# A selective-scan layer with routed experts: a second PSUM bank for the output projection, and turned y in the bank of the inputs' product

## Chip, cores and metric

One core of a Trainium2 chip runs the whole program. The time is the device time in microseconds of one execution, and what is compared is the median of several runs.

## The reference

The input x has 8 sequences of 1024 tokens of 128 features. After a layer norm, a Mamba-2 layer and a mixture of experts read the same normalised xn, and both are added to x. The part that the change touches is the Mamba-2 layer:

```
zxbcdt = norm(xn) @ W_in.T                      # z 256, x 256, B 128, C 128, dt 4 columns
xBC = silu(causal conv with 4 taps of xBC)
Y_diag, states, Y_off = chunked scan over tokens
Y = Y + xs * D                                  # "skip"
y = Y * silu(z)                                 # "gate"
y = y * rsqrt(mean(y * y) + eps) * rms_w
out = y @ W_out.T                               # "output projection"
x = x + (xn + out) + experts(xn)
```

The kernel uses chunks of 128 tokens, so there are 64 tiles of 128 tokens, 8 in each sequence.

## The kernel before

Each engine has its own hand-written program, and semaphores join them. After a prologue (norms, routing, first projection) comes the scan, from about 100 to 490 us, then the experts (500 to 705 us) and the final sum. The scan runs over 8 sequences with a loop for sequences 1 to 6; in each, `sequence(b)` runs over j = 0 to 7, one tile nn = 8b + j each. Four tiles are a group (g = j // 4, q = j % 4): the input projection, convolution and Silu are made for 512 tokens at once, for the next group, while the scan works on the present one.

What the engines do for a tile, in order:

- TensorE: `exponents` (L781, L782) builds the decay exponents in bank 2; `project` (L771) makes one of six blocks of the next group's input projection in bank 0; `front` (L790, L792) the product of B and C and three transposes; `project_out` (L825, L827) multiplies the gated y of tile nn-3 by W_out and sums its squares, all in bank 7; `middle` (L806, L809, L810) makes both parts of y in bank 5 and the inputs' product in the first half of bank 6; `turn_y` (L817) transposes y of tile nn-1 into bank 1. At q = 3 there is no projection, and `project_out` comes first.
- VectorE: `outputs` (L1164, L1167, L1169; L1171 and L1172 for j = 0) takes y and state out of banks 5 and 6; `skip` (L1189) adds D times x to the turned y of tile nn-2; `gate` (L1199) multiplies by silu(z); `by_token` makes `xb` (L1149) and the masked product `m_sb` (L1153); between them lie the other three convolution taps of the next group (L1076), where the table FILL puts them. `outputs` of tile j-1 is called in the quarter of tile j, except that at q = 3 both j-1 and j are done.
- ScalarE: `keep_out` (L604, L605) copies the output projection and the sum of squares out of bank 7 for tile nn-4; `decays` (L566) is the exponential of the exponents; `row` (L597) the row for the experts; `keep_proj` (L534) and `tap0` (L541) copy the projection and make the first tap; `square` (L609) squares the gated y. At the end of q = 2 come `keep_out` of tile nn-3 and then `silu` (L552 to L561), with a load of the activation table on either side.
- POOL scales the inputs (`xde`, L428) and the state (`state_k`, L463) and scatters rows to memory.

Two orders matter. `project_out` waits until the output of the tile before has been copied out of bank 7 (`o_kept`), so at q = 3 and q = 0 it waits for ScalarE's copies on either side of Silu. And `middle` waits for `y_done` of the tile before and for `xde_done`, since it overwrites banks 5 and 6.

Of the kernel before, what the change touches and what calls it, by code (L numbers as in the profile page):

```python
# [27 lines left out]
P = 128  # L28
# [33 lines left out]
def program(nc, x, ln_w, ln_b, w_in_t, w_dt, conv_w, conv_b, dt_bias, a_log, d_skip, rms_w, w_out_t,  # L62
            router, gate_w, up_w, down_w, out):
    ctx = ExitStack()
    with ctx:  # L65
# [3 lines left out]
        def sem(name):  # L69
# [143 lines left out]
        ms_done, rms_sq, rms_done, resid_done, place_free, total_done = (sem(n) for n in (  # L213
            "ms_done", "rms_sq", "rms_done", "resid_done", "place_free", "total_done"))

        def by_head(t):
# [270 lines left out]
        def _(act_e):  # L487
# [111 lines left out]

            def keep_out(nn):  # L600
                act_e.wait_ge(norm_done, 2)
                act_e.wait_ge(o_done, nn + 1)
                act_e.wait_ge(xn_done, nn + 1)
                A(x_sb[:, tile_ix(nn), :].rearrange("p a d -> p (a d)"), bank[7][:, 0:D], ACT.Copy)  # L604
                A(ssq[:, tile_ix(nn)], bank[7][:, D:D + 1], ACT.Copy).then_inc(o_kept, 1)  # L605

# [4 lines left out]
            def sequence(b):  # L611
                first, last = is_first(b), is_last(b)
                for j in range(SC):
                    nn, q, g = b * SC + j, j % GC, j // GC
                    more = not (last and g == 1)
                    nxt, g6 = b * 2 + g + 1, (b * 2 + g + 1) * NAT
                    if q < 3 and not (first and j < 4):
                        keep_out(nn - 4)
# [12 lines left out]
                    if more and q == 2:  # L631
                        keep_proj(g6, 5, 1 - g)
                    if not (first and j < 2):
                        square(nn - 2, j % 2)
                    if more and q == 0:
                        keep_proj(g6, 2, 1 - g)
                    if more and q == 1:
                        tap0(g6, 2, 1 - g)
                        tap0(g6, 3, 1 - g)
                        keep_proj(g6, 4, 1 - g)  # L640
                    if q == 2:
                        if not last:
                            act_e.wait_ge(taps_done, nxt * NCT * HALO + 2 * HALO)
                            halo(nxt + 1, g, 0)
                            keep_proj(g6 + NAT, 0, g)
                            act_e.wait_ge(front_done, nn + 2)
                            tap0(g6 + NAT, 0, g)
                        if more:
                            act_e.wait_ge(m_done, nn + 1)
                            decays(nn + 2, j % 2)  # L650
                        if not (first and j < 4):
                            keep_out(nn - 3)
                        if more:
                            silu(nxt, 1 - g)
                    if last and g == 1 and q:
                        weights_high(q - 1)
# [10 lines left out]
            weights_high(3)  # L667
            keep_out(NT - 4)
            keep_out(NT - 3)
            for n_ in (NT - 2, NT - 1):  # L670
                square(n_, n_ % 2)
            for n_ in (NT - 2, NT - 1):
                keep_out(n_)
            act_e.wait_ge(ms_done, 1)
# [30 lines left out]
        def _(pe):  # L705
# [89 lines left out]
            def middle(b, j):  # L795
# [4 lines left out]
                else:  # L800
                    pe.wait_ge(y_done, nn)
                    if j % GC == 0:
                        pe.wait_ge(m_done, nn + 1)
# [7 lines left out]

            def turn_y(nn, u, early):
                pe.wait_ge(y_done, nn + 1)
                if not early:
                    pe.wait_ge(skip_done, nn)
                for c in range(2):
                    tp = nc.tensor.transpose(bank[1][:, c * P:(c + 1) * P], y_sb[:, u, c * P:(c + 1) * P], ident[:, :])  # L817
                tp.then_inc(yt_done, 1)

            def project_out(nn, u, early):  # L820
                pe.wait_ge(sq_done, nn + 1)
                if not early:
                    pe.wait_ge(o_kept, nn)
                for c in range(2):
                    mm(bank[7][:, 0:D], yg[:, u, c * P:(c + 1) * P], wo_sb[:, c, :], start=(c == 0), stop=(c == 1))  # L825
                for c in range(2):
                    m = mm(bank[7][:, D:D + 1], sq[:, u, c * P:(c + 1) * P], ones[:, 0:1], start=(c == 0),  # L827
                           stop=(c == 1))
# [16 lines left out]
            def sequence(b):  # L845
                first, last = is_first(b), is_last(b)
                for j in range(SC):
# [10 lines left out]
                    if more and q:  # L858
                        project(*nxt, 2 * q + 1)
                    if not (first and j < 3):  # L860
                        project_out(nn - 3, (j - 3) % 2, first and j < 4)
                    if q == 2 and not (last and g == 1):
# [4 lines left out]
                    if not (first and j < 1):  # L867
                        turn_y(nn - 1, (j - 1) % 2, first and j < 2)
                    if ahead and q == 3:
# [5 lines left out]
            project_out(NT - 3, (NT - 3) % 2, False)  # L875
            turn_y(NT - 1, (NT - 1) % 2, False)
            project_out(NT - 2, (NT - 2) % 2, False)
# [65 lines left out]
        def _(dve):  # L943
# [213 lines left out]
            def outputs(b, j):  # L1157

                nn, u, later = b * SC + j, j % 2, b * (SC - 1) + j
                dve.wait_ge(mid_done, nn + 1)  # L1160
                if j:
                    if not (is_first(b) and j == 1):
# [19 lines left out]
            def skip(nn, j):  # L1182
# [5 lines left out]
                for c in range(2):  # L1188
                    sk = V.scalar_tensor_tensor(out=yd_sb[:, c * P:(c + 1) * P], in0=ab[:, XT0 + c, cs],  # L1189
                                                scalar=ds_c[:, c:c + 1], in1=bank[1][:, c * P:(c + 1) * P],  # L1190
                                                op0=ALU.mult, op1=ALU.add)
                sk.then_inc(skip_done, 1)

            def gate(nn, j, group):
                ab, cs, u = group_act(j // GC), in_group(j), j % 2
                dve.wait_ge(skip_done, nn + 1)
                if j % GC == 0:
                    dve.wait_ge(gate_silu, group + 1)
# [13 lines left out]
            def sequence(b):  # L1212
                first, last = is_first(b), is_last(b)
                for j in range(SC):
# [127 lines left out]
```

## Time and profile before

| | |
|---|---|
| median of 3 runs | 753.68 us (751.95 to 761.06) |
| profiled execution | 749.04 us, of which the span of instructions is 747.2 us |
| mean granted TensorE clock | 0.957 |
| busy, share of the span | PE 81%, DVE 77%, ACT 63%, POOL 57% |
| busiest group on DVE | L1076, convolution taps, 192 instructions, 147.6 us |
| chain that ended last | PE 26%, nearly all of it in the experts (L908, L936, L925) |

The trace names the engines PE (TensorE), DVE (VectorE), ACT (ScalarE) and POOL (GpSimd). PEld is TensorE's load of weights. The chain that ended last is followed back from the end and reaches the experts, not the scan; for the scan one has to read waits and timelines.

### The profile page before, as it was taken

How to read it: one execution, taken by the hardware profiler on the slowest of the kernel's cores; microseconds unless marked ns; L12 is line 12 of the kernel's file. 1: busy time of each engine (PE TensorE's matmuls, PEld its weight loads, DVE VectorE, ACT ScalarE, POOL GpSimd, SP SyncE). 2: the span in 40 equal slices, each digit the busy share in tenths (PEclk: the TensorE clock that was granted, in tenths of full speed). 3: DMA queues.
4: the chain of work that ended last, by engine and by line, in shares of the span. 5: the costliest groups of instructions: out<-in, count | busy, mean ns of one | idle time of the engine just before them, and what ended most of it. 6: DMA issues, size and time to landing. Idle time of an engine off the chain costs nothing. (4 is left out here: it accounts for less than half of the span.)

```text
span 747.2 us, 15261 instructions
## 1 busy us (share of the span) xinstructions
PE 608.8 (81%) x3702; PEld 516.1 (69%) x3703; DVE 577.9 (77%) x1440; ACT 470.5 (63%) x1014; POOL 425.8 (57%) x622
## 2 busy tenths in 40 slices
PE   0696448888998999999899988769999999999700
PEld 0696226677877777877777777658898888888600
DVE  7676998998988989889889898766666667666354
ACT  0254355788778887788877887446666666666400
POOL 4343006677767667676777657705666666666710
PEclk9999999999999999899999999979999999999955
DMA  9980000000000000000000003333333333332179
GB/s 304 268 174 0 26 6 17 26 26 29 24 26 27 24 23 23 23 26 27 23 23 27 23 24 111 111 89 105 107 113 105 105 105 109 107 106 81 43 289 385
DMA packets 64651, 61.48 MB, mean 82 GB/s; under 512 B 9242, under 2 KB 55710, under 8 KB 64624
## 3 DMA queue, kind: packets, MB, share of 16 engines
q1 hardware_dynamic: 56176, 44.11, 20.6%
q0 software_dynamic: 8448, 17.06, 6.7%
q8 instruction: 11, 0.18, 0.1%
q14 instruction: 16, 0.13, 0.1%
HBM read 30.19 MB, written 31.47 MB: 83 GB/s over the span
## 5 line engine op out<-in xcount | busy, mean ns | idle before, releaser
L479 POOL DMA_INDIRECT moe_d<-raw,slot_st x136 | 133.7, 983 | 91.9 <-issue 69.4
L452 POOL DMA_INDIRECT slots_d<-rows,slot_st x128 | 135.9, 1062 | 74.1 <-POOL rows L447 52.8
L1076 DVE SCALAR_TENSOR_TENSOR act<-raw,taps,act 128x512 f32<-128x512 f32 x192 | 147.6, 776 | 16.6 <-ACT act L541 15.8
L680 ACT ACTIVATE l_sb<-bank 128x256 f32<-128x256 f32 x136 | 44.8, 381 | 73.2 <-PE bank L908 73.2
L428 POOL TENSOR_TENSOR xde<-xb,e_end 128x256 f32<-128x256 f32 x64 | 48.1, 751 | 62.6 <-DVE xb L1149 61.3
L1264 DVE CAST x_hi<-bank 128x256 fp32r<-128x256 f32 x68 | 28.9, 425 | 64.0 <-PE bank L917 64.0
L806 PE MATMUL bank<-xb,m_sb 128*128 128x64 f32 x512 | 71.4, 285 | 6.5 <-POOL xde L428 4.4
L806 PEld LDWEIGHTS bank<-xb,m_sb 128*128 128x128 f32 x512 | 66.7, 200 | 8.3 <-issue 4.6
L936 PE MATMUL bank<-act,raw 128*128 x544 | 71.9, 275 | 0.0
L936 PEld LDWEIGHTS bank<-act,raw 128*128 128x128 f32 x544 | 66.1, 192 | 0.2 <-issue 0.2
L908 PE MATMUL bank<-xw_hi,x_hi 128*128 x136 | 59.9, 440 | 6.0 <-DVE m_sb L1275 6.0
L825 PE MATMUL bank<-wo_sb,yg 128*128 128x128 f32 x256 | 41.9, 287 | 26.1 <-ACT tok L605 25.7
L534 ACT ACTIVATE raw<-bank,proj_b 128x512 f32<-128x512 f32 x64 | 44.0, 688 | 25.7 <-PE bank L771 22.8
L825 PEld LDWEIGHTS bank<-wo_sb,yg 128*128 128x128 f32 x256 | 36.1, 193 | 34.3 <-issue 20.7
L771 PE MATMUL bank<-xw_hi,w_hi 128*128 (+1 forms) x96 | 51.9, 540 | 5.6 <-ACT raw L534 3.2
L541 ACT ACTIVATE act<-raw,cols,taps 128x512 f32<-128x512 f32 x64 | 50.2, 807 | 8.6 <-DVE meta L1140 5.8
L609 ACT ACTIVATE sq<-yg 128x256 f32<-128x256 f32 x64 | 26.3, 410 | 44.3 <-DVE yg L1199 44.2
L908 PE MATMUL bank<-xw_lo,x_hi 128*128 x136 | 53.9, 396 | 0.0
L908 PE MATMUL bank<-xw_hi,x_lo 128*128 x136 | 53.8, 395 | 0.0
L1153 DVE TENSOR_TENSOR m_sb<-l_sb,bank 128x512 f32<-128x512 f32 x64 | 43.4, 678 | 0.0
L1164 DVE TENSOR_TENSOR yo_sb<-bank,e_cs 128x256 f32<-128x256 f32 x56 | 23.4, 417 | 25.2 <-PE bank L810 25.2
L566 ACT ACTIVATE l_sb<-bank 128x512 f32<-128x512 f32 x64 | 38.2, 597 | 6.6 <-PE bank L782 6.5
(233 smaller groups left out, 1692.8 us busy)
## 6 DMA issues: line engine op xcount, KB each, us to landing
slots_d<-rows SPq DMA_DIRECT2D x8, 1122.0 KB, 13.6
rows<-slots_d SPq DMA_DIRECT2D x68, 132.0 KB, 2.2
x_sb<-in_x SPq DMA_DIRECT2D x8, 512.0 KB, 6.4
act<-in_x SPq DMA_DIRECT2D x64, 64.0 KB
xw_hi<-moe_d SPq DMA_DIRECT2D x8, 512.0 KB, 9.1
xw_lo<-moe_d SPq DMA_DIRECT2D x8, 512.0 KB, 9.8
out<-x_sb SPq DMA_DIRECT2D x8, 512.0 KB, 13.3
moe_d<-raw,slot_st POOLq DMA_INDIRECT x136, 2.3
```

The lines of the kernel that those rows point to most:

```text
L428: nc.gpsimd.tensor_tensor(by_head(xde[:, u, :]), by_head(xdt[:, u, :]), per_head(e_end, nn), ALU.mult).then_inc(xde_done, 1)
L452: nc.gpsimd.indirect_dma_start(out=slots_d, out_offset=bass.IndirectOffsetOnAxis(ap=slot_st[:, r, c:c + 1], axis=0), in_=rows[:, r, c, :], ...
L479: nc.gpsimd.indirect_dma_start(out=moe_d, out_offset=bass.IndirectOffsetOnAxis(ap=slot_st[:, r, c:c + 1], axis=0), in_=ym[r % R][:, c * D: ...
L534: A(proj[:, t, HALO:] if t < NCT else group_act(par)[:, t, :], bank[0][:, :], ACT.Identity, bias=proj_b[:, t:t + 1]).then_inc(proj_done, 1)
L541: A(group_act(par)[:, t, :], proj[:, t, HALO:], ACT.Identity, bias=cb_c[:, t:t + 1], scale=taps[:, t, HALO:]).then_inc(tap0_done, 1)
L680: a = A(l_sb[:, r % 2, c * F:(c + 1) * F], bank[2 + 2 * (r % 2) + c][:, 0:F], ACT.Silu)
L771: m = mm(bank[0][:, :], w[:, c], v[:, bass.ds(b * SW + PADW + half * GT, GT)], start=(a == 0), stop=(a == 2))
L806: mm(bank[5][:, h * HD:(h + 1) * HD], m_sb[:, u, h * P:(h + 1) * P], xdt[:, u, h * HD:(h + 1) * HD], start=True, stop=True)
L825: mm(bank[7][:, 0:D], yg[:, u, c * P:(c + 1) * P], wo_sb[:, c, :], start=(c == 0), stop=(c == 1))
L908: gu = mm(bank[2 + 2 * (r % 2) + c][:, :], xs[:, r % 2, c * P:(c + 1) * P], w[:, bass.ds(ex[c] * (2 * F), 2 * F)], start=(a == 0), stop=(a ...
L936: o = mm(bank[1 + 6 * (r % 2)][:, c * D:(c + 1) * D], ht[r % 2][:, (2 * c + f) * P:(2 * c + f + 1) * P], dn_sb[:, bass.ds(ex[c] * (2 * D) ...
L1076: V.scalar_tensor_tensor(out=group_act(par)[:, t, :], in0=proj[:, t, k:k + GT], scalar=taps[:, t, k:k + 1], in1=group_act(par)[:, t, :], o ...
```

## The change

It gives the output projection two banks, 7 and 1, taken in turn by the parity of the tile, so that `project_out` waits for the copy of the tile two before. Bank 1 came from `turn_y`, whose transposes now go to the second half of bank 6, beside the inputs' product. Since a bank must not be written by TensorE while VectorE reads it, `middle` now waits for `skip` of tile nn-2, `outputs` waits for `turn_y` of the tile before, and `gate` names its wait for the projection that read its buffer. At q = 0 `project_out` moves behind `middle` and `turn_y`, and the `skip` of that quarter moves to the quarter before, between `xb` and the masked product. On ScalarE the copy that stood before Silu moves behind it, after the square.

```
+        out_ps = (bank[7], bank[1])
+        yt_ps = bank[6][:, DI:2 * DI]
...
-            def keep_out(nn):
+            def keep_out(nn, u):
...
-                A(x_sb[:, tile_ix(nn), :].rearrange("p a d -> p (a d)"), bank[7][:, 0:D], ACT.Copy)
+                A(x_sb[:, tile_ix(nn), :].rearrange("p a d -> p (a d)"), out_ps[u][:, 0:D], ACT.Copy)
...
                     if not (first and j < 2):
                         square(nn - 2, j % 2)
+                    if q == 3 and not (first and j < 4):
+                        keep_out(nn - 4, j % 2)
...
-                        if not (first and j < 4):
-                            keep_out(nn - 3)
                         if more:
                             silu(nxt, 1 - g)
...
                     pe.wait_ge(y_done, nn)
+                    if not (is_first(b) and j < 2):
+                        pe.wait_ge(skip_done, nn - 1)
...
-                    tp = nc.tensor.transpose(bank[1][:, c * P:(c + 1) * P], y_sb[:, u, c * P:(c + 1) * P], ident[:, :])
+                    tp = nc.tensor.transpose(yt_ps[:, c * P:(c + 1) * P], y_sb[:, u, c * P:(c + 1) * P], ident[:, :])
...
-                    pe.wait_ge(o_kept, nn)
+                    pe.wait_ge(o_kept, nn - 1)
...
-                    mm(bank[7][:, 0:D], yg[:, u, c * P:(c + 1) * P], wo_sb[:, c, :], start=(c == 0), stop=(c == 1))
+                    mm(out_ps[u][:, 0:D], yg[:, u, c * P:(c + 1) * P], wo_sb[:, c, :], start=(c == 0), stop=(c == 1))
...
-                    if not (first and j < 3):
-                        project_out(nn - 3, (j - 3) % 2, first and j < 4)
+                    if q and not (first and j < 3):
+                        project_out(nn - 3, (j - 3) % 2, first and j < 5)
...
                     middle(b, j)
                     if not (first and j < 1):
-                        turn_y(nn - 1, (j - 1) % 2, first and j < 2)
+                        turn_y(nn - 1, (j - 1) % 2)
+                    if not q and not (first and j < 3):
+                        project_out(nn - 3, (j - 3) % 2, first and j < 5)
...
                 dve.wait_ge(mid_done, nn + 1)
+                if not (is_first(b) and j < 1):
+                    dve.wait_ge(yt_done, nn)
...
                 dve.wait_ge(skip_done, nn + 1)
+                if not isinstance(nn, int) or nn > 1:
+                    dve.wait_ge(o_done, nn - 1)
...
-                    if not (first and j < 2):
+                    if q and not (first and j < 2):
                         skip(nn - 2, (j - 2) % SC)
...
-                    if not (last and j == SC - 1):
+                    if q < 3:
                         by_token(b, j + 1, lambda: fill(2))
+                    elif not (last and j == SC - 1):
+                        by_token(b, j + 1, lambda: skip(nn - 1, j - 1))
+                        fill(2)
```

## Rows read from the trace of the kernel before

**Rows 1.** Busy time by stretch; columns: stretch, PE, PEld, DVE, ACT, POOL, clock, DMA.
```profile
180.00:230.00 50.00, 45.87 (x294) 38.25 (x294) 44.13 (x96) 41.93 (x85) 35.15 (x59) 1.00 0.08 25
```

**Rows 2.** Waits, 180.14 to 271.75 us, four groups: total us, times, longest.
```profile
ACT sq L609 <- DVE yg L1199: 8.5, 8, 1.8
PE bank L825 <- ACT tok L605: 7.6, 8, 1.5
...
DVE act L1076 <- ACT act L541: 4.5, 8, 0.7
DVE yo_sb L1164 <- PE bank L810: 4.5, 4, 1.1
...
ACT raw L534 <- PE bank L771: 3.8, 8, 1.0
```

**Rows 3.** ScalarE's timeline, table load before Silu: start us, length us.
```profile
180.14 1.28 ACT L552 ACT_TABLE_LOAD   x1
...
271.75 1.28 ACT L552 ACT_TABLE_LOAD   x1
295.91 1.28 ACT L552 ACT_TABLE_LOAD   x1
...
436.25 1.28 ACT L552 ACT_TABLE_LOAD   x1
```

**Rows 4.** ScalarE's timeline through one group; in brackets the idle time before.
```profile
245.90 0.42 ACT L609 ACTIVATE sq<-yg 128x256 f32<-128x256 f32 x1 [1.29 <-DVE yg L1199]
...
257.10 0.81 ACT L541 ACTIVATE act<-raw,cols,taps 128x512 f32<-128x512 f32 x1
```

**Rows 5.** VectorE's timeline through the same group.
```profile
248.84 0.41 DVE L1169 TENSOR_TENSOR y_sb<-yo_sb,bank 128x256 f32<-128x256 f32 x1
249.17 0.60 DVE L1189 SCALAR_TENSOR_TENSOR yd_sb<-act,cols,bank 128x128 f32<-128x128 f32 x2
...
252.01 0.42 DVE L1164 TENSOR_TENSOR yo_sb<-bank,e_cs 128x256 f32<-128x256 f32 x1 [1.12 <-PE bank L810]
...
254.14 0.68 DVE L1153 TENSOR_TENSOR m_sb<-l_sb,bank 128x512 f32<-128x512 f32 x1
...
257.94 1.56 DVE L1076 SCALAR_TENSOR_TENSOR act<-raw,taps,act 128x512 f32<-128x512 f32 x2 [0.41 <-ACT act L541]
...
261.68 0.50 DVE L1199 TENSOR_TENSOR yg<-yd_sb,act 128x256 f32<-128x256 f32 x1
```

**Rows 6.** TensorE's timeline: the first group's q = 3, then the same group.
```profile
132.95 1.10 PE L806 MATMUL bank<-xb,m_sb 128*128 128x64 f32 x8 [1.02 <-DVE y_sb L1169]
...
248.98 0.68 PE L825 MATMUL bank<-wo_sb,yg 128*128 128x128 f32 x4 [0.95 <-ACT tok L605]
...
249.86 1.08 PE L806 MATMUL bank<-xb,m_sb 128*128 128x64 f32 x8
...
251.27 0.59 PE L810 MATMUL bank<-xde,xb 128*128 128x256 f32 x2
251.70 0.38 PE L817 MATMUL bank<-ident,y_sb 128*128 128x128 f32 x2
...
255.28 0.71 PE L825 MATMUL bank<-wo_sb,yg 128*128 128x128 f32 x4 [0.66 <-ACT tok L605]
...
256.20 1.08 PE L806 MATMUL bank<-xb,m_sb 128*128 128x64 f32 x8
...
257.75 0.48 PE L771 MATMUL bank<-xw_hi,w_hi 128*128 x1
```

**Rows 7.** POOL's timeline: inputs scaled for the first tile of a group.
```profile
253.75 0.95 POOL L428 TENSOR_TENSOR xde<-xb,e_end 128x256 f32<-128x256 f32 x1 [0.69 <-DVE xb L1149]
```

**Rows 8.** TensorE's timeline and stretch (clock ahead of the last two), slow group; tail.
```profile
272.76 1.62 PE L806 MATMUL bank<-xb,m_sb 128*128 128x64 f32 x8
...
274.00:278.00 4.00, 4.00 (x16) 3.07 (x16) 1.65 (x5) 3.97 (x7) 1.65 (x2) 0.68 0.11 34
...
489.98 1.19 PE L825 MATMUL bank<-wo_sb,yg 128*128 128x128 f32 x4 [0.57 <-ACT tok L605]
```

More of the change, by code:

```diff
@@ L603, in keep_out @@
                 act_e.wait_ge(xn_done, nn + 1)
-                A(x_sb[:, tile_ix(nn), :].rearrange("p a d -> p (a d)"), bank[7][:, 0:D], ACT.Copy)
-                A(ssq[:, tile_ix(nn)], bank[7][:, D:D + 1], ACT.Copy).then_inc(o_kept, 1)
+                A(x_sb[:, tile_ix(nn), :].rearrange("p a d -> p (a d)"), out_ps[u][:, 0:D], ACT.Copy)
+                A(ssq[:, tile_ix(nn)], out_ps[u][:, D:D + 1], ACT.Copy).then_inc(o_kept, 1)
             def square(nn, u):
@@ L617, in sequence @@
                     if q < 3 and not (first and j < 4):
-                        keep_out(nn - 4)
+                        keep_out(nn - 4, j % 2)
                     if q < 3:
@@ L634, in sequence @@
                         square(nn - 2, j % 2)
+                    if q == 3 and not (first and j < 4):
+                        keep_out(nn - 4, j % 2)
                     if more and q == 0:
@@ L667, in _ @@
             weights_high(3)
-            keep_out(NT - 4)
-            keep_out(NT - 3)
+            keep_out(NT - 4, 0)
+            keep_out(NT - 3, 1)
             for n_ in (NT - 2, NT - 1):
@@ L672, in _ @@
             for n_ in (NT - 2, NT - 1):
-                keep_out(n_)
+                keep_out(n_, n_ % 2)
             act_e.wait_ge(ms_done, 1)
@@ L810, in middle, with turn_y @@
                 mm(bank[6][:, 0:DI], b_sb[:, u, :], xde[:, u, :], start=True, stop=True).then_inc(mid_done, 1)
-            def turn_y(nn, u, early):
+            def turn_y(nn, u):
                 pe.wait_ge(y_done, nn + 1)
-                if not early:
+                if not isinstance(nn, int) or nn > 0:
                     pe.wait_ge(skip_done, nn)
                 for c in range(2):
-                    tp = nc.tensor.transpose(bank[1][:, c * P:(c + 1) * P], y_sb[:, u, c * P:(c + 1) * P], ident[:, :])
+                    tp = nc.tensor.transpose(yt_ps[:, c * P:(c + 1) * P], y_sb[:, u, c * P:(c + 1) * P], ident[:, :])
                 tp.then_inc(yt_done, 1)
@@ L822, in project_out @@
                 if not early:
-                    pe.wait_ge(o_kept, nn)
+                    pe.wait_ge(o_kept, nn - 1)
                 for c in range(2):
-                    mm(bank[7][:, 0:D], yg[:, u, c * P:(c + 1) * P], wo_sb[:, c, :], start=(c == 0), stop=(c == 1))
+                    mm(out_ps[u][:, 0:D], yg[:, u, c * P:(c + 1) * P], wo_sb[:, c, :], start=(c == 0), stop=(c == 1))
                 for c in range(2):
-                    m = mm(bank[7][:, D:D + 1], sq[:, u, c * P:(c + 1) * P], ones[:, 0:1], start=(c == 0),
+                    m = mm(out_ps[u][:, D:D + 1], sq[:, u, c * P:(c + 1) * P], ones[:, 0:1], start=(c == 0),
                            stop=(c == 1))
@@ L875, in _ @@
             project_out(NT - 3, (NT - 3) % 2, False)
-            turn_y(NT - 1, (NT - 1) % 2, False)
+            turn_y(NT - 1, (NT - 1) % 2)
             project_out(NT - 2, (NT - 2) % 2, False)
@@ L1189, in skip @@
                     sk = V.scalar_tensor_tensor(out=yd_sb[:, c * P:(c + 1) * P], in0=ab[:, XT0 + c, cs],
-                                                scalar=ds_c[:, c:c + 1], in1=bank[1][:, c * P:(c + 1) * P],
+                                                scalar=ds_c[:, c:c + 1], in1=yt_ps[:, c * P:(c + 1) * P],
                                                 op0=ALU.mult, op1=ALU.add)
```

## The prediction, as it was made before the changed kernel ran

> **What bounds the kernel now.** I looked first at busy time by stretch. In the scan, where the whole change lies, TensorE is busy 45.9 of 50 us, VectorE 44.1 and ScalarE 41.9, at a granted clock of 1.00 [rows 1]. Nobody is far from full, so a stall on one engine proves nothing about the span; what sets the pace has to be found as a closed loop.
>
> The second view is the waits over four groups of four tiles [rows 2]. TensorE stalls 7.6 us in 8 places, two per group, before the output projection (L825), released each time by ScalarE's copy of the squares' sum (L605). That is the stall the change goes after: 1.9 us per group. But ScalarE waits 8.5 us for VectorE's gate (L1199), and VectorE 4.5 us for ScalarE's first tap (L541) and 4.5 us for TensorE's L810, the latter once per group.
>
> The third view gives the pace. The table load before Silu comes once per group: at 180.14 and four groups later at 271.75, that is 22.90 us per group; the next comes 24.16 us later. From 180.14 to 436.25 there are eleven groups in 256.11 us, 4.2 more than 11 x 22.90; three slow groups make up the difference [rows 3].
>
> The fourth view is the two engines' timelines through one group [rows 4, 5]. Read it from ScalarE's squaring at 245.90, which waited 1.29 us for VectorE's gate. Between it and the tap of 257.10 to 257.91 lie 20 instructions, and the view names no idle time before any of them: halo, projection copy, tap, decays, a late output copy, both table loads and three Silus, square, another output copy, decays, row, halo and projection copy. VectorE's two taps start at 257.94, right behind it, having waited 0.41 us. VectorE then runs to the gate of 261.68 to 262.18; ScalarE squares and makes the next tap; VectorE takes it (the second of its two waits of up to 0.7 us per group [rows 2]) and runs to the gate one period after 245.90. This loop goes VectorE, ScalarE, VectorE, ScalarE. It does not pass through TensorE. TensorE's stalls, 0.95 us at 248.98 and 0.66 us at 255.28 [rows 6], are slack which it has in every group.
>
> **The change part by part.** *Stall before the third-quarter projection (q = 3).* With two banks, project_out of tile T waits for the copy of T-2, which ScalarE makes a whole quarter earlier. So at q = 3 the four plus four matmuls follow the transposes at once; they took from 248.98 to 249.86 [rows 6], so, started at 248.98 - 0.95 = 248.03, they end at 248.91, and 0.95 us is freed. What is late next is middle(). It already needs y (written 248.84 to 249.25), and now also skip(), since bank 6 holds both the transposed y and the inputs' product. Skip's two instructions ended at 249.17 + 0.60 = 249.77 [rows 5]. From y's end to a waiting middle() took 0.05 us or less in the first group, where it started at 132.95 [rows 6]. So middle() starts at 249.8 to 249.9, against 249.86 before: worth 0. The freed 0.95 us becomes a stall on skip.
>
> Here the Trainium skill bears on it: its page "PSUM — Partial Sum Buffer", section "PSUM bank collisions raise a hardware error", says that two engines may not touch one bank in the same partitions at once even at different columns, so the new wait cannot be dropped. No row shows a collision. By the page's rule middle() is worth 0 as above; without the shared bank y alone would hold it and it would start 0.5 us sooner.
>
> *Outputs wait for the transposes.* VectorE's outputs() now also waits for turn_y() of the tile before. At q = 3 that is directly behind middle(): L810 ends at 251.27 + 0.59 = 251.86, L817 at 251.70 + 0.38 = 252.08 [rows 6], so the y sequence that started at 252.01 starts 0.22 us later. Behind it on VectorE stand xb, skip, the masked product and two taps, then gate, xb and product of the next quarter. The 0.41 us before 257.94 [rows 5] covers it: 0.19 is left and the cost is 0. Without that cover it would be 0.22 x 14 groups = 3 us. At q = 1 and 2 VectorE waits for L810 nowhere, since there is one such wait per group [rows 2], so there it is hidden.
>
> *Skip moved.* In the last quarter skip takes the place of a tap between xb and the masked product, and the tap follows. The two skip instructions take 0.60, a tap 0.78 (two in 1.56 at 257.94) [rows 5]. The product started at 254.14; now it starts no later than 254.14 + 0.22 = 254.36 and ends near 255.0; xde on POOL, 253.75 to 254.70 before [rows 7], ends near 254.9. Middle() at q = 0 starts there, after the fronts that end at 255.28 - 0.66 = 254.62 [rows 6], where it started at 256.20 before. The projection moved behind it pays its 0.92 us (255.28 to 256.20) later. From middle() to project(2) it is 1.55 us (256.20 to 257.75), so project(2) starts at 255.0 + 1.55 + 0.92 = 257.5, against 257.75: some 0.3 us sooner. Nothing in the loop wants that: ScalarE, which copies this projection, then waits for a gate anyway. VectorE's sum of work is the same; price 0.
>
> *Late copy behind Silu.* The pair L604, L605 leaves the place before the table load, and Silu starts sooner by its time. Then the same pair stands behind the square, with the q = 0 pair after it. ScalarE reaches decays(), row() and the tap of 257.10 [rows 4] after exactly the same instructions: 0. The projection at q = 0 waits for the copy that now ends near 254.9, while TensorE comes to it near 256.5: no wait. The copies of q = 0 need the projection of q = 3, done at 249. The gate's new wait, on a projection that ended quarters ago (257.4 for the gate of 261.68), is free too.
>
> *Waits as instructions.* Four more waits per group on VectorE, one or two on TensorE. No row shows a bubble for one on VectorE, where instruction follows instruction in the loop. Bounds: nothing, or 0.05 us each, the smallest gap that any row here shows, for the two or three of them that lie in the loop: 0 to 0.15 us per group, 0 to 2 us. I take 0.
>
> *First group.* At q = 3 middle() waited 1.02 us for y with no output copy in the way [rows 6]. Now it waits for skip: +0.5, and with the transposes +0.2. VectorE then runs on without a wait, so this counts: +0.7.
>
> *Clock.* At 272.76 the eight matmuls of middle() take 1.62 us where they take 1.08 at 249.86; the granted clock of 274 to 278 is 0.68, so part of it lies at 1.2 and not 2.4 GHz, and this follows the stall of q = 3 [rows 8]. The group is 24.16 us long, 1.26 more, so TensorE has entered the path there and the 0.41 us of cover is used up. In such a group the transposes cost their slow length, twice the 0.22 us of above or 0.43, all of it on the path: 3 x 0.43 = +1.3.
>
> *Tail.* The last projection waited 0.57 us for the copy of the one before [rows 8]; with its own bank it doesn't: -0.6.
>
> Sum: 0 + 0.7 + 1.3 - 0.6 = +1.4 us on this execution's 749.04 us. The median of the three runs is 753.68, 4.6 above it; I carry the difference over: 753.68 + 1.4 = 755.1 us. About 2%, 15 us, is what a measurement can tell from no change.
>
> **The rivals.** *A, TensorE is in the loop after all.* For it: TensorE is the busiest engine, and ScalarE waits 3.8 us for projections (L771) in these four groups [rows 2]. Against it: ScalarE's waits for the gate that follow are over twice as long (8.5 us), and the stall at q = 3 changes from group to group, up to 1.5 us, while the period doesn't move. If so, the 1.9 us of stalls per group would all count: 14 groups x 1.9 = 27, time 727.
>
> *B, the clock falls more often.* The change gathers TensorE's idle time at q = 3: freed work makes it come 0.3 us sooner and leave at the same time, so 0.95 grows to about 1.2. The slow stretch of [rows 8] began there. Against it: the four groups of [rows 2] had stalls of up to 1.5 us and kept their 22.90 us. If it fell in all 16 groups, 13 more x (1.26 + 0.43) = +22 us: 777. It decides from 9 more on (9 x 1.69 = 15 us). The Trainium skill, "TensorE: Matmul & The Clock Gate", section "HAM oscillation — how this bites in real kernels", says that waits between bursts of matmuls throw the clock back again each time; that is this rival, and the trace agrees in 3 groups and not in the rest.
>
> *C, the new waits outgrow the 0.41 us.* If a wait for skip costs 0.2 and one for the transposes 0.4 instead of 0.22, 0.2 to 0.4 us per group show: 16 x 0.3 = 5, time 760.
>
> *D, the slow stretches go.* If TensorE's idle is better placed now, 4.2 + 1.3 us fall away: 755.1 - 5.5 = 749.6.
>
> **Chances.** Forecast 0.55, C 0.15, D 0.12, A 0.10, B 0.08. Leaving out A and B, the range goes from D less the spread of the runs (752 to 754) to C plus a few slow stretches: 745 to 764. Faster by over 2% is A (0.10), slower is B (0.08), within 2% the rest (0.82).
>
> **What would show it.** Right: table loads still 22.9 us apart; L825 no longer waits for L605; TensorE waits instead for L1189 (skip) before L806 at q = 3, about 1 to 1.5 us per group; VectorE's wait for L810 near 1.3 and its wait at 257.94 near 0.2; ScalarE's waits for the gate as before. Wrong: a period below 22.5 (A) or above 23.2 with VectorE's taps no longer waiting for L541 at q = 0 (C); more tenths of granted clock under 9 (B).

## The result, and the profile after

The changed kernel takes 761.31 us (median of 18 runs, 755.15 to 765.42), the kernel before 755.49 us on the same chips (18 runs, 750.51 to 761.06): ratio 1.0077, 95% interval 1.0052 to 1.0102. The forecast was 755.1 us within 745 to 764, and "within 2%"; both hold. Within the range, though, it lies 6.2 us on the slow side. Of these, 1.8 are the kernel before, which took 755.49 us here and not 753.68; the rest is that the change costs 5.8 us where +1.4 was forecast. Most of this document is about those 5.8 us. The ratios here and below leave out executions over 1.5% above the fastest of their kernel, such as one of b_fill_tail at 830.6 us and one of a_pool at 2038.6.

| | before | after |
|---|---|---|
| span of the profiled execution | 747.2 us | 761.3 us |
| mean granted TensorE clock | 0.957 | 0.936 |
| second to third table load (the first full group) | 25.11 us | 28.07 us |
| the 13 groups after it | 300.93 us | 308.30 us |
| last table load to the end of the span | 289.0 us | 291.9 us |

The profiled execution of after is 14 us longer than that of before, more than twice what the medians say: before's was one of its fastest. Its mean clock of 0.957 is as high as the highest of 29 executions of before in the second series below (0.933 to 0.957, the middle one 0.945). Two more profiles of the changed kernel (below) have 305.50 and 305.70 us in the 13 groups. I use these as typical.

Of what the prediction said would show its steps right, most is there. The waits over four groups, the answer to [rows 2] (columns: total us, times, longest):

```profile
ACT sq L612 <- DVE yg L1210: 11.1, 8, 2.1
DVE yo_sb L1173 <- PE bank L815: 9.2, 4, 3.3
...
PE bank L811 <- DVE yd_sb L1198: 5.4, 3, 2.1
```

The wait of the output projection (now L830) for ScalarE's copy (now L608) is gone from the list, 7.6 us before. In its place TensorE waits for VectorE's skip (yd_sb) ahead of middle. It names three of the four groups; the stall of the fourth, 1.1 us, stands in the list under the y (L1178) that VectorE writes just before. The timeline shows the single stalls. TensorE around the last quarter, q = 3, of a group with a long one, the answer to [rows 6]:

```profile
230.56 0.61 PE L830 MATMUL bank<-wo_sb,yg 128*128 128x128 f32 x4
231.01 0.51 PE L832 MATMUL bank<-ones,sq 128*128 128x1 f32 x4
233.58 1.89 PE L811 MATMUL bank<-xb,m_sb 128*128 128x64 f32 x8 [2.07 <-DVE yd_sb L1198]
...
353.13 1.08 PE L811 MATMUL bank<-xb,m_sb 128*128 128x64 f32 x8 [1.39 <-DVE yd_sb L1198]
```

The output projection runs right behind the transposes, and middle (L811) waits 2.07 us. Its eight matmuls then take 1.89 us, against 1.08 in the last row, after a stall of 1.39. That is the clock, in the answer to [rows 8] (stretch; busy us of PE, PEld, DVE, ACT, POOL with counts; granted clock; DMA):

```profile
232.00:236.00 4.00, 2.42 (x10) 2.36 (x11) 2.57 (x7) 3.97 (x6) 2.39 (x7) 0.71 0.05 16
236.00:240.00 4.00, 4.00 (x14) 2.77 (x13) 2.08 (x7) 2.92 (x8) 1.10 (x2) 0.50 0.10 34
```

A granted clock of 0.50 is the lower of the two levels, 1.2 GHz. The group that follows is 24.91 us long. VectorE waits 3.31 us for L815 there, where a group at full clock looks like this (VectorE's timeline, the answer to [rows 5]):

```profile
355.55 0.42 DVE L1173 TENSOR_TENSOR yo_sb<-bank,e_cs 128x256 f32<-128x256 f32 x1 [1.39 <-PE bank L815]
...
358.13 1.53 DVE L1083 SCALAR_TENSOR_TENSOR act<-raw,taps,act 128x512 f32<-128x512 f32 x2
359.58 0.53 DVE L1210 TENSOR_TENSOR yg<-yd_sb,act 128x256 f32<-128x256 f32 x1
...
361.21 1.54 DVE L1083 SCALAR_TENSOR_TENSOR act<-raw,taps,act 128x512 f32<-128x512 f32 x2
```

The wait for L815 is 1.39 (predicted 1.3), the taps at 361.21 wait for nobody (predicted 0.2 left), and this group is 22.84 us long against 22.90: close to the forecast. But it is the only one of the 13 apart from the last, whose load comes early in both kernels (22.82 here, 21.99 before), that is below 23.2. Before, nine of 13 were at 22.8 to 22.9 [rows 3]. Why the others are longer is the question.

### The profile page after: what moved, and what is told of

It reads as the page before. It is cut to its first block, busy times and chain, and to the rows that moved or that the text cites. A ratio compares the mean times of both kernels' runs of the same rounds, so it can differ in the third digit from the quotient of the medians.

```text
span 761.3 us, 15330 instructions
## 1 busy us (share of the span) xinstructions
PE 622.4 (82%) x3702; PEld 527.7 (69%) x3703; DVE 581.3 (76%) x1440; ACT 471.0 (62%) x1014; POOL 421.1 (55%) x622
## 4 chain that ended last, share of the span: by engine, by line
PE 67%; DVE 18%; issue 7%; DMA 3%; POOL 1%; SPq 1%; ACT 1%; DVEq 0%; POOLq 0%; ACTq 0%
PE bank L915 13%; PE bank L811 8%; PE bank L774 7%; PE bank L943 7%; PE bank L932 4%; PE bank L815 3%; PE bank L728 3%; PE bank L814 3%; PE bank L784 3%; DVE act L1083 2%; PE bank L830 2%; PE bank L785 2%; PE bank L718 2%; PE bank L924 2%; DMA xw_lo<-moe_d 2%
## 5 line engine op out<-in xcount | busy, mean ns | idle before, releaser
L455 POOL DMA_INDIRECT slots_d<-rows,slot_st x128 | 137.9, 1078 | 74.0 <-POOL rows L450 52.8
L1083 DVE SCALAR_TENSOR_TENSOR act<-raw,taps,act 128x512 f32<-128x512 f32 x192 | 151.2, 795 | 13.2 <-ACT act L544 11.8
L811 PE MATMUL bank<-xb,m_sb 128*128 128x64 f32 x512 | 72.3, 288 | 32.7 <-DVE yd_sb L1198 20.3
L811 PEld LDWEIGHTS bank<-xb,m_sb 128*128 128x128 f32 x512 | 67.8, 203 | 37.7 <-DVE y_sb L1178 25.7
L431 POOL TENSOR_TENSOR xde<-xb,e_end 128x256 f32<-128x256 f32 x64 | 41.6, 650 | 76.1 <-DVE xb L1156 74.9
L612 ACT ACTIVATE sq<-yg 128x256 f32<-128x256 f32 x64 | 26.3, 411 | 49.5 <-DVE yg L1210 49.3
L815 PE MATMUL bank<-xde,xb 128*128 128x256 f32 x128 | 44.1, 430 | 0.0
L814 PE MATMUL bank<-state,act 128*128 128x256 f32 x112 | 41.2, 454 | 0.0
```

The costliest lines, as they stand in the source:

```text
L455: nc.gpsimd.indirect_dma_start(out=slots_d, out_offset=bass.IndirectOffsetOnAxis(ap=slot_st[:, r, c:c + 1], axis=0), in_=rows[:, r, c, :], ...
L811: mm(bank[5][:, h * HD:(h + 1) * HD], m_sb[:, u, h * P:(h + 1) * P], xdt[:, u, h * HD:(h + 1) * HD], start=True, stop=True)
L814: mm(bank[5][:, DI:2 * DI], group_act(j // GC)[:, CT, in_group(j)], state[:, :], start=True, stop=True)
L815: mm(bank[6][:, 0:DI], b_sb[:, u, :], xde[:, u, :], start=True, stop=True).then_inc(mid_done, 1)
L1083: V.scalar_tensor_tensor(out=group_act(par)[:, t, :], in0=proj[:, t, k:k + GT], scalar=taps[:, t, k:k + 1], in1=group_act(par)[:, t, :], o ...
```

## The experiments

All ratios are to the kernel before, run on the same chip in the same series. There were three series. In the first the chip is one on which the kernel before takes 791.7 us, nearly all of the extra time in the experts (334.1 us from the last table load to the end in the first experiment's profile, against 289.0), so ratios of that series are compared with each other alone. In the second before takes 755.37 us, in the third 753.74. The ratios are those of the record; they aren't quotients of the medians, and differ from these by up to some 0.004 (b_fill_tail_2: 0.9822 recorded, 743.44 / 753.74 = 0.9863). The profile of each run, one execution, gives two sums that are free of the experts: the first full group, and the 13 groups after it.

| kernel | series | ratio, 95% interval | clock | first group | 13 groups |
|---|---|---|---|---|---|
| before | | 1 | 0.957 | 25.11 | 300.93 |
| b_waits | 1 | 1.0015 (0.9983 to 1.0046) | 0.931 | 30.58 | 299.07 |
| b_fill | 1 | 0.9923 (0.9888 to 0.9958) | 0.948 | 25.30 | 297.03 |
| a_fill | 1 | 1.0022 (0.9982 to 1.0062) | 0.939 | 28.07 | 300.45 |
| a_skip_back | 1 | 1.0151 (1.0104 to 1.0198) | 0.927 | 29.73 | 309.32 |
| a_plain | 2 | 1.0078 (1.0047 to 1.0108) | 0.936 | 28.45 | 305.50 |
| b_skip_moved | 2 | 1.0045 (1.0012 to 1.0077) | 0.947 | 25.38 | 304.01 |
| a_fill_pool | 2 | 0.9965 (0.9934 to 0.9997) | 0.960 | 26.65 | 299.19 |
| b_fill_tail | 2 | 0.9854 (0.9809 to 0.9900) | 0.969 | 25.12 | 296.79 |
| a_pool | 3 | 1.0068 (1.0027 to 1.0108) | 0.935 | 28.33 | 305.54 |
| a_plain_2 | 3 | 1.0063 (1.0023 to 1.0104) | 0.938 | 27.13 | 305.70 |
| a_best | 3 | 0.9933 (0.9899 to 0.9967) | 0.968 | 27.85 | 299.57 |
| b_fill_tail_2 | 3 | 0.9822 (0.9764 to 0.9879) | 0.969 | 25.13 | 296.95 |

Names with a stand for the changed kernel with an edit, those with b for the kernel before with one. The clock is the mean of the profiled execution, the last two columns are us. The profile of b_waits is that of its longest execution, 798.75 us where its median is 790.10. Every interval lies within 2% of 1 but that of b_fill_tail_2, which spans the 2%. In the expectations one theory puts the loss down to TensorE's clock, which falls after the gathered stall at q = 3; a second, formed after the first series, to VectorE and POOL holding each other up once skip has moved; a third to the waits themselves.

**The waits alone (b_waits).** Only the two new waits, in the kernel before:

```
+ middle:  if not (is_first(b) and j < 2): pe.wait_ge(skip_done, nn - 1)
+ outputs: if not (is_first(b) and j < 1): dve.wait_ge(yt_done, nn)
```

> The kernel before with only two waits added: middle waits for skip of tile nn-2, outputs waits for the transposes of the tile before. Banks and orders as before. Theory W (the new waits are what makes the change slower): about the change's own loss, ratio 1.005 to 1.008, groups of 23.3 us. Theory K (the loss comes mainly from more and longer stretches at half clock, since the change gathers TensorE's idle time in one stall at q = 3): here ScalarE's late copy still splits the idle time, skip is finished when TensorE comes, and the 0.41 us of cover takes the 0.22 us of the transposes; ratio 1.000 to 1.003.

Measured 1.0015, no difference. The groups at full clock are 22.86 to 22.96 us long, so four more wait instructions per group on VectorE and the order they impose cost nothing there. That settles rival C too: VectorE waits 1.39 us for the inputs' product (at 328.00) and no longer for the first tap at q = 0, so the cover is used up as in the changed kernel, and the period stays. The first group is another matter: 30.58 us against 25.11. Its TensorE timeline has, at q = 3,

```profile
134.43 1.63 PE L808 MATMUL bank<-xb,m_sb 128*128 128x64 f32 x8 [1.62 <-DVE yd_sb L1193]
```

a stall of 1.62 us for skip where before waited 1.02 for y [rows 6], and then half clock: 1.63 us for what took 1.10. In all, 5.5 us are lost once in this one profile, the longest execution; three of the 13 groups have a mean granted clock of 0.93, as against 0.93, 0.86 and 0.93 before, and the 13 take 1.9 us less.

**TensorE kept busy in the stall (b_fill, a_fill).** Extra matmuls, whose result nobody reads, at q = 3 of each group but those of the last sequence: in b_fill three ahead of project_out, in a_fill four behind it and ahead of middle. a_skip_back is the changed kernel with the skip of q = 0 back in its old place, behind the last tap of the quarter before.

```
+ if q == 3 and not last:
+     for i in range(4):   # 3 in b_fill
+         mm(bank[0][:, :], w_hi[:, 0:P], xw_hi[:, bass.ds(b * SW + PADW, GT)], start=True, stop=True)
```

> The kernel before with three extra matmuls (128 x 512, results unused, in bank 0) ahead of project_out at q = 3, where TensorE stalls 0.95 to 1.5 us; the extra work takes about 0.7 us. Theory K: with less idle time the clock falls less often, the 4 us of slow groups go, ratio 0.992 to 0.997, mean clock above 0.957. Theory W says nothing on clock: the extra work lies in a stall, ratio 1.000, slow groups as often as before.

> The changed kernel with four such matmuls behind project_out at q = 3, ahead of middle, where it stalls 1.1 to 2.1 us on skip; the extra work takes about 0.95 us. Theory K: the slow stretches go, clock back to 0.955 or more, ratio to the kernel before 0.995 to 1.001. Theory W: the waits stay as they are, ratio 1.005 to 1.008.

> The changed kernel with skip of q = 0 back in its old place, behind the last taps of the quarter before, so middle at q = 0 waits for it there. Expected by the prediction's steps: middle at q = 0 starts near 256.0 instead of 254.9 in the old count, about 1 us later, project_out behind it, so project(2) comes 1 us later than in the kernel before and ScalarE's copy of it reaches into its wait for the gate (0.3 to 0.8 us of slack): 0.2 to 0.6 us per group, 3 to 9 us slower than the changed kernel, ratio 1.011 to 1.02. If the moved skip is itself the harm (its place changes how VectorE and POOL meet), it is faster than the changed kernel, ratio 1.000 to 1.005.

b_fill gains 0.8%: its 13 groups take 297.03 us, 3.9 less than before's, and all but the last lie between 22.85 and 22.94. So the three slow groups of [rows 3] come from the clock, and 4 us were to be had in the kernel before for matmuls that compute nothing. a_fill loses its clock-slowed groups too (305.6 to 300.45), and is still 3.4 us behind b_fill in the 13 groups, at a granted clock of 1.00 in both. Between the two the ratios differ by 0.0099, no less than the 0.0077 between the kernels without filler. So the clock theory, on its own, falls: by it the two with extra matmuls would be equal. a_fill's table loads show what is left (ScalarE's timeline; start, length):

```profile
323.59 1.28 ACT L555 ACT_TABLE_LOAD   x1
347.03 1.28 ACT L555 ACT_TABLE_LOAD   x1
369.87 1.28 ACT L555 ACT_TABLE_LOAD   x1
```

23.44 and 22.84 us, in strict turn from 254.46 on: the group that runs into the second half of a sequence (to j = 4) is 0.54 us too long, the one to j = 0 is not. The two halves differ on POOL, which scales the state (state_k) ahead of the token rows for j = 4 and has nothing to scale for j = 0. (VectorE has three instructions in outputs for j = 4 and two for j = 0. That is no rival: before has them too, and its groups are alike.) VectorE and POOL of a_fill at the start of a group to j = 4:

```profile
329.82 1.92 DVE L1090 SCALAR_TENSOR_TENSOR act<-raw,taps,act 128x512 f32<-128x512 f32 x2
...
336.80 0.97 DVE L1217 TENSOR_TENSOR yg<-yd_sb,act 128x256 f32<-128x256 f32 x1
```

```profile
329.80 0.60 POOL L466 TENSOR_TENSOR state_k<-state,e_tot 128x256 f32<-128x256 f32 x1
331.24 0.65 POOL L450 COPY rows<-rows 128x128 f32<-128x128 f32 x1 [0.83 <-ACT rows L600]
332.71 1.03 POOL L455 DMA_INDIRECT slots_d<-rows,slot_st  x1 [0.83 <-POOL rows L450]
334.05 1.46 POOL L455 DMA_INDIRECT slots_d<-rows,slot_st  x1 [0.30 <-issue]
...
336.23 0.69 POOL L442 COPY slot_st<-slot_i 128x2 int32 x1
336.89 0.60 POOL L466 TENSOR_TENSOR state_k<-state,e_tot 128x256 f32<-128x256 f32 x1
```

POOL's state_k starts at 329.80, 0.02 us ahead of the two taps, and these take 1.92 us instead of 1.53 (358.13 above). Further on, one indirect DMA takes 1.46 instead of 0.97, POOL comes late to its copy (0.69 us for one that takes 0.18) and to the next state_k, and the gate that meets this state_k takes 0.97 instead of 0.50. In before, at the same place, the masked product stands between the two taps, skip behind the second, and POOL is the one that waits:

```profile
324.90 0.74 DVE L1076 SCALAR_TENSOR_TENSOR act<-raw,taps,act 128x512 f32<-128x512 f32 x1
...
326.16 0.76 DVE L1076 SCALAR_TENSOR_TENSOR act<-raw,taps,act 128x512 f32<-128x512 f32 x1
326.84 0.59 DVE L1189 SCALAR_TENSOR_TENSOR yd_sb<-act,cols,bank 128x128 f32<-128x128 f32 x2
...
333.10 0.50 DVE L1199 TENSOR_TENSOR yg<-yd_sb,act 128x256 f32<-128x256 f32 x1
```

```profile
326.33 1.05 POOL L463 TENSOR_TENSOR state_k<-state,e_tot 128x256 f32<-128x256 f32 x1
```

Its state_k comes 0.17 us behind the tap, takes 1.05 us, and VectorE loses nothing. The taps and the gate read two tensors from SBUF. Skip and the products with a bank read one from PSUM, and none of these was seen lengthened (skip 0.59 to 0.61 us for its two instructions from 180 to 455 us of before and of a_fill). That is the rule of the Trainium skill, "SBUF — State Buffer", section "Who interferes with whom": VectorE's second SBUF input goes through a port pair shared with GpSimd, under an exclusive lock, and "Issue order, not op shape, decides who blocks." This trace agrees, with 1.92 and 0.60 in one order and 0.76 and 1.05 in the other.

Two groups to j = 0 of a_fill show the gate's part by itself. In the first (231.00 - 207.79 = 23.21 us) an indirect DMA took 1.33 us, in the second (277.31 - 254.46 = 22.85 us) 0.97:

```profile
218.18 1.33 POOL L455 DMA_INDIRECT slots_d<-rows,slot_st  x1 [0.30 <-issue]
219.53 0.62 POOL L431 TENSOR_TENSOR xde<-xb,e_end 128x256 f32<-128x256 f32 x1
...
220.87 0.60 POOL L466 TENSOR_TENSOR state_k<-state,e_tot 128x256 f32<-128x256 f32 x1
...
264.55 0.97 POOL L455 DMA_INDIRECT slots_d<-rows,slot_st  x1 [0.30 <-issue]
265.55 0.62 POOL L431 TENSOR_TENSOR xde<-xb,e_end 128x256 f32<-128x256 f32 x1
...
266.38 0.60 POOL L466 TENSOR_TENSOR state_k<-state,e_tot 128x256 f32<-128x256 f32 x1
```

```profile
219.76 1.10 DVE L1090 SCALAR_TENSOR_TENSOR act<-raw,taps,act 128x512 f32<-128x512 f32 x1
220.79 0.97 DVE L1217 TENSOR_TENSOR yg<-yd_sb,act 128x256 f32<-128x256 f32 x1
...
266.42 1.11 DVE L1090 SCALAR_TENSOR_TENSOR act<-raw,taps,act 128x512 f32<-128x512 f32 x1
267.45 0.50 DVE L1217 TENSOR_TENSOR yg<-yd_sb,act 128x256 f32<-128x256 f32 x1
```

In the second, state_k starts 0.04 us ahead of a tap; in the first 0.08 us after the gate has begun, and the gate takes 0.47 longer. (VectorE's starts in this view overlap the end of the instruction before by some 0.08 us, so which came first isn't to be read from it to that accuracy.) The group grows by 0.36. So a lengthened gate is worth some 0.36 us, and the taps about 0.2, the rest of the 0.54.

a_skip_back came out at 1.0151, as expected: with skip behind its taps, middle at q = 0 waits 1.7 to 1.8 us for it, ScalarE waits up to 2.5 us for the projection behind, and groups are 24.00 and 23.5 us long. Here no gate takes over 0.43 us and no pair of taps over 1.53, so the 0.5 us by which these groups alternate isn't the hold-up; no run shows what it is. Since the turned y shares a bank with the inputs' product, skip has to move or middle waits for it; that is what the hold-up was bought for.

**Skip alone, and POOL's order (a_plain, b_skip_moved, a_fill_pool).** In b_skip_moved only the skip of q = 0 stands between xb and the masked product at q = 3. In a_fill_pool a_fill's POOL prepares the token rows ahead of state_k at j = 4.

```
  prepare_ids(b, j)
+ if j == GC: prepare_rows(b, j)      # GC = 4
  if j: state_k ...
- prepare_rows(b, j)
+ if j != GC: prepare_rows(b, j)
```

> The changed kernel once more, on the chip of this set, so that the next ones stand beside it. Ratio to the kernel before 1.005 to 1.010. By the theory that the loss has two parts (groups to j = 4 that are 0.5 us longer, because VectorE's taps and gate collide with POOL's state product, and more groups that lose 1.2 us to the half clock) its groups at full clock alternate between about 22.85 and 23.4.

> The kernel before with only skip of q = 0 moved into the quarter before, between xb and the masked product; banks, waits and all else as before. Theory P: two taps now stand together where a tap and skip stood, POOL's state product gets in ahead of them in the groups to j = 4, which become 23.2 to 23.5 us long, others stay at 22.9: +2 to +4 us, ratio 1.002 to 1.006. Rival (the price lies in banks and waits): all groups 22.9, ratio 0.998 to 1.001.

> The changed kernel with the four extra matmuls at q = 3, and POOL at j = 4 makes the row copy before the state product instead of after it. Theory P (the groups of 23.44 us come from POOL's state product, which starts just before VectorE's two taps at q = 0 and holds them up 0.39 us, and then meets the gate): the 23.44 groups fall to 22.85 to 23.0, 7 groups x 0.5 us = 3 to 4 us less than the earlier one with extra matmuls alone (1.0022), so ratio 0.996 to 1.000. Rival (the 0.5 us is TensorE's waits or one vector operation more at j = 4): the groups still alternate by 0.4 to 0.6 us, ratio 1.001 to 1.003.

b_skip_moved is 1.0045: 3.4 us of the 5.8 come with this one move (0.9 to 5.8 by the interval; the medians are 2.2 apart), its first group is near before's (25.38) and the 13 take 3.1 us more. The hold-up is there with no bank or wait changed:

```profile
233.45 1.93 DVE L1076 SCALAR_TENSOR_TENSOR act<-raw,taps,act 128x512 f32<-128x512 f32 x2
```

```profile
233.44 0.60 POOL L463 TENSOR_TENSOR state_k<-state,e_tot 128x256 f32<-128x256 f32 x1
```

Two of its groups to j = 4 run at full clock, and are 23.23 and 23.22 us long; those to j = 0 at full clock are at 22.84 to 22.90. So the hold-up alone costs 0.3 us where it strikes, or 2 us in all. In the changed kernel at full clock it is 0.54 us, most likely since there the waits have used up the cover already. The rest of the 3.1 us goes with the clock: 7 of the 13 groups have a mean granted clock of 0.93, against 3 in the profile of before, whose mean clock is a high one.

a_fill_pool's ratio of 0.9965 is as the hold-up theory said, but a_fill was run on another chip, and a_fill_pool's trace shows less. The taps at the start take 1.53 us in every group, and the groups to j = 4 have fallen from 23.44 to 23.22. But the gate of these still takes 0.97 us, behind an indirect DMA of 1.38. So the turned order took away 0.22 of the 0.54 us, 1.3 us in the 13 groups (300.45 to 299.19), not all of it. That is still the test of the cause: where state_k was moved away, the taps went back from 1.92 to 1.53 us and the groups got shorter.

**POOL's order alone (a_pool, beside a_plain_2).** No filler.

> The changed kernel with only POOL's order in the first tile of a second group turned (token rows before the state's scaling), no extra matmuls. If the hold-up between POOL and VectorE and the fall of the clock are two separate costs, this takes away the first alone: about 7 groups x 0.54 = 3.8 us, so a ratio of 1.0025 (1.001 to 1.005) to the kernel before, a mean clock still near 0.94, groups that are not slowed by the clock near 22.9 and some that are. If the clock alone makes the change slow, nothing is gained: 1.007 to 1.009. If the hold-up was also what made TensorE's stall long enough for the clock to fall, both go: 1.000 or below, with the clock back near 0.957.

> The changed kernel once more, to stand beside a_pool on one chip: 1.005 to 1.010 to the kernel before, mean clock near 0.94.

Measured 1.0068 beside 1.0063, and 305.54 beside 305.70 us in the 13 groups: nothing gained, where 1.0025 was expected. The 1.3 us are within the intervals; beyond that, a_pool's groups are 23.2 to 24.98 long and of the 13 only one is at 22.9 (and the last). In eight of these groups the clock falls. The 3.8 us expected had counted the gate's part in, which the turned order doesn't remove; 1.3 us, or 0.0017, was all there was to gain, and this run can't tell it from nothing. Whether the two costs simply add up stays open.

**TensorE kept busy in the last group too (b_fill_tail, a_best).** Small extra matmuls (the identity by ones, 128x128) at q = 3, in the last group and behind the last projections; a_best is a_fill_pool with those of the end.

```
+ for i in range(k):   # k = 2, 3, 9 in the last group, 6, 2, 2, 4 behind it
+     mm(bank[0][:, 0:P], ident[:, :], ones[:, :], start=True, stop=True)
```

> The kernel before with three extra matmuls (128 x 128 in two passes, about 0.7 us together) at q = 3 in the sequences 0 to 6, and as many as fit into TensorE's stalls in the last group and in the change from the scan to the experts (2, 3, 9, 6, 2, 2 and 4 of them). Theory K: groups of 22.9 us without exception as with the earlier three (0.992), and the clock stays at 1.00 also from the scan's end to the experts' start, where it was 0.64 to 0.67 for 20 us: 2 to 5 us more, ratio 0.985 to 0.991. If the clock there doesn't answer to such work, ratio 0.991 to 0.995; if the extra work gets in the way, above 0.995.

> The kernel before with small extra matmuls in the last quarter's stall and in the last group and behind the last projections, once more, to stand beside a_best on one chip: 0.984 to 0.989 as in its first run; at or a little below a_best, since no hold-up between POOL and VectorE stands in it and the steady groups of both are 22.9 us.

> The changed kernel with the extra matmuls in the stall of the last quarter, POOL's turned order, and extra small matmuls in the last group and behind the last projections. By the theory that TensorE's clock is the remaining cost: 0.9965 for the first two, and another 0.005 to 0.009 for the last group and what follows it, so 0.9875 to 0.9915. If the extra matmuls of the tail only lengthen it: 0.997 or above. If the second bank for the output projection is worth something once TensorE keeps its clock, it beats the kernel before with the same extra matmuls (b_fill_tail_2, on this chip) by 0.001 or more; if it is worth nothing, the two agree within 0.002 or the changed one is behind.

b_fill_tail beats both kernels: 743.44 to 743.98 us, 0.9822 and 0.9854. a_best, at 748.36 us, is 4.9 us behind it on the same chip (expected up to 0.9915 for it, measured 0.9933). The clock is held in the 13 groups and nearly so behind them in both, but not in the first group of a_best (mean 0.88 there, 1.00 in b_fill_tail_2). So this is what the change costs with POOL's order turned, the first group's clock included. In the two profiles (748.0 and 741.8 us) the 6.2 us lie in the first group (27.85 - 25.13 = 2.7), in the 13 groups (299.57 - 296.95 = 2.6) and, with 0.6, ahead of the first group; from the last table load to the end both take 287.6 to 287.8 us.

## Why the prediction was right, and where it was not

*What bounds the kernel.* Right. A stall of 1.9 us per group went, and nothing was gained, so rival A is out. The group that nothing disturbs is 22.84 us long.

*Stall at q = 3 turned into a wait for skip.* Right in kind: L830 no longer waits, middle waits for yd_sb. The size was under-read: 1.39 us in an undisturbed group, within the 1 to 1.5 named, but up to 2.07 in others.

*Outputs wait for the transposes, covered by 0.41 us.* Right: VectorE's wait for the inputs' product went from 1.12 [rows 5] to 1.39, and b_waits' groups stayed at 22.87. In the changed kernel the gate in front of the cover takes 0.53 instead of 0.42, so not 0.19 but next to nothing of it is left. The prediction's own sign for rival C (periods above 23.2, no wait for the first tap at q = 0) is there, and C's time, 760 us, is close to the measured one; b_waits shows all the same that the waits alone don't lengthen the group. They matter in that a later delay is no longer covered.

*"Skip moved … VectorE's sum of work is the same; price 0."* This is the step that failed. The sum of work was the same, the durations were not: with skip in the first tap's place two taps lie back to back behind the masked product, and POOL's state_k, until then delayed by a tap, comes first. At held clock the changed kernel loses 300.45 - 297.03 = 3.4 us in the 13 groups; the move alone (b_skip_moved) costs 0.45%, 3.4 us too, of which some 2 us are the hold-up at full clock. The rows that would have told it stood in the trace of before: state_k at 1.05 us in some places and 0.60 in others, the tap at 0.74 and 1.16.

*First group, +0.7.* Mis-sized. The first full group grew by 2.0 to 3.3 us in three profiles without filler. The middle's wait grew by 0.59 (1.02 to 1.61), as predicted, but the clock falls behind it. Two rows of after:

```profile
134.38 1.70 PE L811 MATMUL bank<-xb,m_sb 128*128 128x64 f32 x8 [1.61 <-DVE yd_sb L1198]
...
136.00:140.00 4.00, 4.00 (x17) 2.99 (x17) 1.65 (x5) 3.81 (x8) 1.71 (x3) 0.74 0.10 34
```

b_waits has it (in its longest execution) and b_skip_moved does not, as far as one profile each goes, so it comes with the waits. Filling the stall at q = 3 did not cure it: in a_fill this middle is at full clock (1.08), but the granted clock falls at 148 to 156 us instead (0.55 and 0.60), and the group keeps its 28.07 us (26.65 in a_fill_pool, 27.85 in a_best).

*Clock, 3 x 0.43 = +1.3.* The mechanism (slow transposes on the path) wasn't separated. What the runs show is what the half clock takes in the 13 groups: 3.9 us before (300.93 - 297.03), 5.1 to 5.3 in the typical profiles after (305.50, 305.70 - 300.45), a difference of 1.2 to 1.4. The profile of after that came with the result has 7.9. As before's own profiled execution was one of its fastest, the difference may be smaller still. Rival B, that the clock falls more often, is true of the profiles: 6 to 8 of the 13 groups have a granted clock under 1.00, against 3. But that is 3 to 5 more and not the 9 from which B decides. B's reason, the gathered idle time, isn't shown: b_skip_moved, whose stall at q = 3 is where it was, has 7 such groups. D, that they go, is out.

*Tail, -0.6.* The wait for the copy is gone: the projection at 502.38 waits 0.40 us for ScalarE's square (L612), not for a copy. But nothing of it reached the end. From the last table load to the end the three profiles are 0.9 to 3.6 us longer than before's 289.0, and with the tail filled the two kernels agree.

*Late copy behind Silu, waits as instructions: 0.* Nothing speaks against it; b_waits shows it for the waits. The late copy wasn't tried alone.

*The sum.* First group 2.0 to 3.3, skip 3.4, clock at most 1.4, make 5.4 to 8.1 us; measured 5.8. It is a rough sum, as each term comes from one or a few profiles. The forecast had +1.4. It was right on the class and the range since none of these terms is large, not because its terms were; and that the range reached to 764 is owed to C and a few slow stretches, so that 761 lies in it is in part luck.

*Open.* Why the indirect DMA on POOL takes 1.33 to 1.46 us and not 0.97 in some groups: those of a_fill at 218.18 and 334.05 lie over a pair of VectorE's taps, but so does that of 264.55, which takes 0.97, and no run changed that alone. And why the first group loses a stretch of clock even with its first stall filled.

## What to carry to other kernels

When an instruction is moved on VectorE, its own cost may be the same and that of its neighbours not: look at what it stood between, where their operands lie (SBUF or PSUM), and what POOL starts there. A duration that differs between two places of one profile (0.60 and 1.05 us for the same scaling) marks such a meeting, and should be priced before the order is changed. And where the granted clock dips behind a stall of 1.5 to 2 us, put spare matmuls into the stall before reworking who waits for whom: here that was worth 10 to 11 us in all (743.44 beside 753.74, 743.98 beside 755.37), and the rework cost 6. The profiles show 5.9 us of that gain (spans of 747.2 and 741.3 us, 4.1 in the 13 groups and 1.4 from the last table load on), and the execution of before among them, at 749.04 us, is itself 4 to 6 us under the medians; no profile places the rest.

## What the hardware showed that I had not expected

- TensorE's clock fell towards the lower level behind single stalls of 1.45 to 2.1 us in a stretch in which it is otherwise busy 46 of 50 us [rows 1]. The length of the stall alone doesn't decide it: in the kernel before, one of 1.45 us was followed by the slow middle of [rows 8], one of 1.46 two groups earlier was not (nor was one of 1.97 at 185.66 in a_plain):

```profile
226.07 0.68 PE L825 MATMUL bank<-wo_sb,yg 128*128 128x128 f32 x4 [1.46 <-ACT tok L605]
...
271.88 0.68 PE L825 MATMUL bank<-wo_sb,yg 128*128 128x128 f32 x4 [1.45 <-ACT tok L605]
```

- Three matmuls of 128x512 or three of 128x128 in the stall kept each of the first 12 of the 13 groups at 22.8 to 22.9 us in the kernel before.
- Kept in the last group and behind it, the clock was worth another 2.1 us (289.9 to 287.8 us from the last table load to the end, a_fill_pool to a_best), and 1.4 in the kernel before (289.0 to 287.6).
- One instruction of POOL that starts 0.02 us ahead of two taps of VectorE lengthens them by 0.39 us; one that starts 0.17 us behind is itself delayed, by 0.45 us (1.05 for 0.60). A copy of 128x2 numbers on POOL took 0.17 to 0.19 us in most places and 0.69 where it began 0.12 us behind a tap of VectorE (336.23 and 336.11 in a_fill).
